# Reordering the merge of a triangular inverse: both halves' steps one and two first, then step three of the second half alternating with step four of the first

## The reference, cut to what matters

```python
M = jnp.tril(M, k=-1)
kexp = kg * jnp.exp(Gg)[:, :, :, None, :]
rhs = (vg - jnp.einsum('bhtid,bhdv->bhtiv', kexp, S)).reshape(b, h, C * Rr, dv)
u = jax.scipy.linalg.solve_triangular(M, rhs, lower=True, unit_diagonal=True)
...
S_new = jnp.exp(glast)[..., None] * S + jnp.einsum('bhtid,bhtiv->bhdv', kdec, u)
```

## Time and profile before

| | |
|---|---|
| runs of the kernel | 5012.32, 5018.0, 5028.32 us (median 5018.0) |
| span of the profiled execution | 5005.7 us |
| PE busy | 4517.9 us (90%), 63200 matmul records |
| PE weight loads | 3131.9 us (63%), beside the matmuls |
| DVE busy | 4134.4 us (83%) |
| ACT busy | 3484.7 us (70%) |
| POOL busy | 3217.8 us (64%) |
| DMA | mean 27 GB/s, queue 1 at 7.2% of 16 engines |

### The profile page before, as it was taken

How to read it: one execution, slowest core, us unless ns; L and a number is a source line. 1 busy time by engine, 2 the same in 40 slices (tenths; PEclk the granted TensorE clock), 3 DMA queues, 4 the chain that set the end, 5 groups by cost and what they waited for, 6 DMA issues and landing times.

```text
span 5005.7 us, 151432 instructions
## 1 busy us (share of the span) xinstructions
PE 4517.9 (90%) x63200; PEld 3131.9 (63%) x63200; DVE 4134.4 (83%) x7262; ACT 3484.7 (70%) x6775; POOL 3217.8 (64%) x5316
## 2 busy tenths in 40 slices
PE   8869999999999999999999999899999999999888
PEld 5536666666666666666666666666666666666655
DVE  3289998888988899889998899888998899988622
ACT  3367777777777777777777777777777777777531
POOL 0047777776777777777777777777777777777600
PEclk9979999999999999999999999999999999999899
DMA  2200000000000000000100000000000000000100
GB/s 88 94 21 21 25 25 25 16 22 25 34 32 15 28 25 25 25 14 25 34 32 28 15 25 25 25 16 23 30 29 25 14 24 25 25 25 8 38 9 21
DMA packets 49724, 135.45 MB, mean 27 GB/s; under 512 B 7056, under 2 KB 28176, under 8 KB 48400
## 3 DMA queue, kind: packets, MB, share of 16 engines
q1 hardware_dynamic: 49040, 125.77, 7.2%
HBM read 111.60 MB, written 14.16 MB: 25 GB/s over the span
## 4 chain that ended last, share of the span: by engine, by line
PE 54%; DVE 26%; ACT 11%; issue 7%; POOL 1%; DMA 0%; DVEq 0%; SPq 0%; ACTq 0%
PE bank L835 46%; DVE acc L1557 8%; PE bank L302 7%; DVE X L1554 7%; DVE sp_t L1554 2%; ACT L1432 2%; DVE Pd L1662 2%; ACT Us L1181 2%; ACT o L1182 1%; DVE Zc L1741 1%; DVE Rs L1557 1%; DVE o L1557 1%; ACT acc L1181 1%; PE bank L906 1%; DVE x1m L1554 1%
## 5 line engine op out<-in xcount | busy, mean ns | idle before, releaser
L1557 DVE SCALAR_TENSOR_TENSOR acc<-bank,vc,acc 128x510 f32<-128x510 f32 (+2 forms) x1728 | 1272.9, 740 | 148.5 <-ACT acc L1181 122.9
L2002 POOL TENSOR_TENSOR LZ<-LZ,LT 128x120 f32<-128x120 f32 (+26 forms) x1984 | 957.3, 483 | 155.5
L1999 POOL TENSOR_TENSOR LT<-LA,LZ 128x120 f32<-128x120 f32 (+26 forms) x1984 | 917.1, 462 | 145.9
L1554 DVE TENSOR_TENSOR X<-KQ,Fl 128x640 f32<-128x640 f32 x1024 | 1002.8, 995 | 1.5 <-ACT Fl L1182 1.5
L1972 POOL COPY X<-KQ 128x640 f32<-128x640 f32 x256 | 246.4, 962 | 912.4 <-PE bank L835 312.2
L835 PE MATMUL bank<-X 128*32 128x60 f32 (+1 forms) x32768 | 650.8, 205 | 132.6 <-DVE Pd L1662 85.9
L835 PEld LDWEIGHTS bank<-X 128*32 128x32 f32 x32768 | 524.7, 112 | 369.1 <-issue 211.0
L1181 ACT ACTIVATE Us<-bank 128x128 f32<-128x128 f32 x1024 | 281.2, 276 | 621.3 <-PE bank L835 615.2
L835 PE MATMUL bank<-xnTm,WK 128*128 128x512 f32 x1280 | 662.7, 643 | 42.0 <-DVE acc L1557 36.3
L835 PE MATMUL bank<-Rs,Ztf 128*128 128x128 f32 x2048 | 467.4, 314 | 68.8 <-DVE Rs L1557 48.6
L1951 POOL TENSOR_TENSOR kdec<-KQ,Fe 128x512 f32<-128x512 f32 x256 | 336.8, 1316 | 299.4 <-PE bank L906 299.4
(11 more groups left out here) (145 smaller groups left out, 9346.4 us busy)
## 6 DMA issues: line engine op xcount, KB each, us to landing
WK<-in_wkq SPq DMA_DIRECT2D x64, 704.0 KB, 5.9
WV<-in_wv SPq DMA_DIRECT2D x64, 576.0 KB, 3.8
WO<-in_wo SPq DMA_DIRECT2D x64, 128.0 KB, 2.0
wuh<-in_wu SPq DMA_DIRECT2D x2, 1024.0 KB, 7.4
xt<-in_x SPq DMA_DIRECT2D x4, 512.0 KB, 6.2
wuh_d<-wuh SPq DMA_DIRECT2D x1, 2048.0 KB, 6.3
x_d<-x SPq DMA_DIRECT2D x4, 512.0 KB, 3.1
xnT_d<-xT SPq DMA_DIRECT2D x4, 512.0 KB, 2.7
```

What stands on the lines that cost most here:

```text
L1554: return e.tensor_tensor(o, a, b, op)
L1557: return e.scalar_tensor_tensor(out=o, in0=a, scalar=sc, in1=b, op0=op0, op1=op1)
L1999: e.tensor_tensor(tmp, LA[:, j + 1:32, 8 * (j % R) + j // R].unsqueeze(2).broadcast_to([P, rr, cc]), LZ[:, j, 0:cc].unsqueeze(1).broadcast ...
L2002: e.tensor_tensor(LZ[:, j + 1:32, 0:cc], LZ[:, j + 1:32, 0:cc], tmp, SUB).then_inc(g_row, 1)
```

## The change

On PE and on ACT the calls of the merge for stage `p-2` stand in another order; `third` and `fourth` on PE become three functions, one of which, `third_fourth`, issues a matmul of the third step of half 1 and one of the fourth step of half 0 in turn. The waits are written anew for this order. What is computed, the number of matmuls, their shapes and the copies on ACT are the same. DVE, GpSimd and the queues are not edited.

```diff
                 w.wait_ge(a_E, every(s, 8))
-                w.wait_ge(a_Z, nth(s, 2, hb - 1))
-                w.wait_ge(a_Y4, nth(s, 2, hb - 1))
+                w.wait_ge(a_Z, every(s - 1, 2))
+                w.wait_ge(a_W, nth(s, 6, 3 * hb - 1))
...
                 w.wait_ge(a_Ys, nth(s, 2, hb))
+                w.wait_ge(a_W, nth(s, 6, 3 * hb - 1))
...
+            def third_of(s, u):
+                return mm(bank[4][64:128, 64 * (u % 8):64 * (u % 8) + 64],
+                          E[0:64, s % 2, u, 1:3].rearrange("p g c -> p (g c)"), Zc[0:64, u, :])
+
+            def fourth_of(s, u):
+                return mm(bank[4][0:64, 64 * (u % 8):64 * (u % 8) + 64], Y4[64:128, u % 8, :], Ztf[64:128, u, 64:128])
+
+            def third(s):
...
+                w.wait_ge(a_W, every(s, 6))
                 for c in range(8):
-                    u = 8 * hb + c
-                    ins = mm(bank[4][64:128, 64 * c:64 * c + 64], E[0:64, s % 2, u, 1:3].rearrange("p g c -> p (g c)"),
-                             Zc[0:64, u, :])
+                    ins = third_of(s, c)
                 ins.then_inc(p_inv[2], 1)
...
+            def third_fourth(s):
...
+                w.wait_ge(a_Y4, nth(s, 2, 0))
                 for c in range(8):
-                    u = 8 * hb + c
-                    ins = mm(bank[4][0:64, 64 * c:64 * c + 64], Y4[64:128, c, :], Ztf[64:128, u, 64:128])
+                    ins = third_of(s, 8 + c)
+                    if c == 7:
+                        ins.then_inc(p_inv[2], 1)
+                    ins = fourth_of(s, c)
+                ins.then_inc(p_inv[3], 1)
+
+            def fourth(s):
...
+                w.wait_ge(a_Y4, every(s, 2))
+                w.wait_ge(a_Z, nth(s, 2, 0))
+                for c in range(8):
+                    ins = fourth_of(s, 8 + c)
                 ins.then_inc(p_inv[3], 1)
```

The list on PE (the list on ACT has the same moves, with `third(p - 2, 1)` and `fourth(p - 2, 0)` where PE has `third_fourth`):

```diff
                 products(p - 1, 2, 4)
-                third(p - 2, 0)
+                first(p - 2, 1)
                 spare(p - 2, 32)
                 turn_v(p - 2, 2)
                 turn(p - 1, 0)
-                fourth(p - 2, 0)
+                second(p - 2, 1)
                 spare(p - 2, 33)
                 total(p)
                 turn_v(p - 2, 3)
                 products(p - 1, 3, 0)
-                first(p - 2, 1)
+                third(p - 2)
                 spare(p - 2, 34)
                 products(p - 1, 3, 1)
                 turn(p - 1, 1)
-                second(p - 2, 1)
+                third_fourth(p - 2)
                 spare(p - 2, 35)
                 products(p - 1, 3, 2)
                 products(p - 1, 3, 3)
                 solve(p - 2, 0, 0)
                 products(p - 1, 3, 4)
                 project_k(p + 1, 0)
-                third(p - 2, 1)
+                fourth(p - 2)
                 spare(p - 2, 36)
                 update(p - 2, 0, 0)
                 project_k(p + 1, 1)
-                fourth(p - 2, 1)
```

ACT's copies of `first` and `third` get one wait more each, for the PE group that still reads `Ys` or `Y4`:

```diff
                 w.wait_ge(p_inv[0], nth(s, 2, hb))
+                w.wait_ge(p_inv[1], nth(s, 2, hb - 1))
...
                 w.wait_ge(p_inv[2], nth(s, 2, hb))
+                w.wait_ge(p_inv[3], nth(s, 2, hb - 1))
```

More of the change, by code:

```diff
@@ L966, in second @@
                 ins.then_inc(p_inv[1], 1)
-            def third(s, hb):
+            def third_of(s, u):
[4 more added lines that the diff above has]
+            def third(s):
                 if not 0 <= s < NS:
                     return
-                w.wait_ge(a_W, nth(s, 6, 3 * hb + 2))
+                w.wait_ge(a_W, every(s, 6))
                 for c in range(8):
-                    u = 8 * hb + c
-                    ins = mm(bank[4][64:128, 64 * c:64 * c + 64], E[0:64, s % 2, u, 1:3].rearrange("p g c -> p (g c)"),
-                             Zc[0:64, u, :])
+                    ins = third_of(s, c)
                 ins.then_inc(p_inv[2], 1)
-            def fourth(s, hb):
+            def third_fourth(s):
                 if not 0 <= s < NS:
                     return
-                w.wait_ge(a_Y4, nth(s, 2, hb))
+                w.wait_ge(a_Y4, nth(s, 2, 0))
                 for c in range(8):
-                    u = 8 * hb + c
-                    ins = mm(bank[4][0:64, 64 * c:64 * c + 64], Y4[64:128, c, :], Ztf[64:128, u, 64:128])
+                    ins = third_of(s, 8 + c)
[4 more added lines that the diff above has]
+            def fourth(s):
+                if not 0 <= s < NS:
+                    return
+                w.wait_ge(a_Y4, every(s, 2))
+                w.wait_ge(a_Z, nth(s, 2, 0))
+                for c in range(8):
+                    ins = fourth_of(s, 8 + c)
                 ins.then_inc(p_inv[3], 1)
@@ L1507, in delta_scalar @@
                 silu_v(p - 1, 2)
-                first(p - 2, 1)
+                third(p - 2, 0)
                 rhs(p - 2, 0, 0)
@@ L1514, in delta_scalar @@
                 turned(p - 1, 1)
-                second(p - 2, 1)
+                third(p - 2, 1)
+                fourth(p - 2, 0)
                 root(p, 1)
@@ L1520, in delta_scalar @@
                 tap_k(p + 1, 0)
-                third(p - 2, 1)
+                fourth(p - 2, 1)
                 factors(p, 0)
```

## The result

The changed kernel takes 5200.9 us (median of 4 runs, 5197.87 to 5218.64) against 5016.3 us: a ratio of 1.0369, 95% interval 1.0345 to 1.0394, slower. The forecast was 5170 us, 5085 to 5235. The profiled execution took 5202.57 us at a span of 5200.7, 195.0 more than the span before.

A forecast was written before the change was run, and what follows sets the result against it. No engine bounds the whole; who waits last at each place counts. 63 steps x 2.2 = 139 us on the 5005.7 span, plus 12.3 for the median and 13 for the clock, gives 5170 us, range 5085 to 5235.

The forecast's parts named there:

- PE ahead of products(3,0) is covered: PE reaches products(3,0) 0.88 us sooner but waits for DVE's `Pd`; idle grows from 1.43 to 2.3 us, worth nothing.
- ACT sets the start of solve(0,0): ACT's four steps take 5.25 us before solve(0,0) is released, so PE waits there 1.6 to 2.5 us.
- The alternating group at 1.3 us, between 1.26 and 2.14: Time on PE of third(1) alternating with fourth(0); the sum does not depend on where in these bounds it lies.
- +2.2 us a stage: DVE empties products(3,4) 2.2 us later, shifting `Rs`; all engines leave the place about 2.2 us late, 139 us over 63 steps.
- The other way through the stage: With fourth(1) ahead of update(0,0) and the second projection, rhs(0,1) and solve(1,0) come 1.9 to 2.2 us later.
- The clock: 8 more falls, 13 us: Two PE idle waits within 7 us cause 8 more costly clock falls, 13 us; bounds none to 101 us.
- The rival of a fall in nearly every stage: Two long waits close together make the clock fall in nearly every stage: plus 101 us, 5258 us; chance 0.10.
- PE's saving: Rival: ACT does not hold solve(0,0), so PE's saving gains 0.52 us a stage: 4985 us; chance 0.06.
- Half absorbed: Rival: DVE or ACT regain about 1.1 us a stage: 5087 us; chance 0.09.
- The order holds the solve: Denied by the no-change rival: the order does not hold solve(0,0), ACT's wait being met earlier, 5018 us; chance 0.04.
- 1.9 a stage without a fall: Low end of the forecast's own range, 5130 us: only PE's shift at solve(1,0) counts and no clock fall.

The follow-up runs named there:

- e1_two_blocks: The changed kernel, but the eight matmuls of third(1) come first and then the eight of fourth(0), not in turn: 5230.5 us.
- e3_copies_first: The changed kernel with ACT's copies of third(1) and fourth(0) moved ahead of the table load, first root and kdT: 5067.1 us.
- e2_solve_behind: The changed kernel with solve(0,0) moved behind products(3,4) on PE: 5127.6 us.
- e5_fill_both: The changed kernel with added matmuls nobody reads, eight ahead of products(3,0) and eleven ahead of solve(0,0): 5175.4 us.
- e7: The kernel before in its own order, with one added wait of solve(0,0) on PE for ACT's second root: 5337.9 us.
- e8_late_early: The changed kernel with both repairs, solve(0,0) behind products(3,4) on PE and ACT's two copies ahead of the table load: 5087.6 us.

## Why the prediction was right, step by step

- *PE ahead of products(3,0) is covered.* Right: 2.06 us of idle time (2.3 forecast), still behind `Pd`, and products(3,0) keeps its place in the stage. PE comes 0.63 us earlier and not 0.88, as a wait of 0.20 us for DVE's `acc` now stands further ahead in its list; that is worth nothing either way.
- *ACT sets the start of solve(0,0).* Right, and shown by two runs: lengthening PE's part moves nothing (steady stage of e1_two_blocks), shortening ACT's part by 2.0 us brings solve(0,0) forward by 2.0 (e3_copies_first). ACT's 5.25 us measured 5.39 (2134.41 to 2139.80), for its unchanged piece took 3.51 us instead of 3.37; solve(0,0) starts 7.13 us after products(3,0), forecast 6.98. PE idles 2.70 us there, a little over the 1.6 to 2.5 forecast.
- *The alternating group at 1.3 us, between 1.26 and 2.14.* It took 1.08, below the lower bound. That bound took the time of the first step as proportional to its columns; sixteen matmuls of 32 columns take 0.63 us and sixteen of 64 columns 1.08, less than twice as long. The sum didn't hang on it. The Trainium skill, "TensorEngine Tiling (Array Packing)", restrictions and gotchas, says that different row tiles cannot access one PSUM bank at the same time. If that is taken to mean that such matmuls run one after the other, it does not hold here, where the two of a pair write different partition halves of bank 4: 1.08 us for sixteen matmuls, against 1.07 for eight of the same size in one tile.
- *+2.2 us a stage.* Mis-sized by 0.26: +2.46. Of it 0.15 is the later release and 0.10 the step from solve(0,0) to products(3,4), taken at 0.32 and measured at 0.42 (2140.22 - 2139.80), for which the forecast had named 0.17 as the risk. 155 us instead of 139. DVE's idle time ahead of products(3,4) was forecast at about 2 us and measured 3.44: DVE was ready 1 us earlier than before (its `rn<-C` ends 4.90 us after products(3,0), before 5.94), as the `X` operation ahead of it took 0.79 us, before 1.83. GpSimd's `kdec` ran beside nearly all of the longer one and beside little of the shorter one; no run changes that alone. It too only lengthened a wait. The other way through the stage came out as forecast: rhs(0,1) starts 13.58 us after products(3,0), forecast 13.5 to 13.7, before 11.40. e2_solve_behind shows that this way costs 1.56 us a stage even where DVE isn't held at products(3,4).
- *The clock: 8 more falls, 13 us.* This is the term that was sized worst. Net 25 more falls in 58 stages (47 against 22), and stages 0.52 us further above their steady length, 33 us in all; e5_fill_both, which takes 33 of the early falls away, wins 26. The forecast took the projection 5 us behind the old wait as the nearest row, where one wait stood and now there are two. Early falls are 5 with 1.43 us at products(3,0) alone, 26 with 2.04 and 0.72 at solve(0,0), 36 with 2.04 and 2.18, 42 with 2.06 and 2.70, and 59 with 1.43 and 3.39 (the kernel before, e3, e2, the changed kernel, e7). But with one of the two filled they are still 37 or 46, so the sum of the waits isn't the rule; which rule holds is open. The rival of a fall in nearly every stage was right in the count, 40 of 58 stages with a fall in that part, and three times too dear, 101 us. Two reasons are likely, neither shown: falls went away elsewhere (17 to 5), and part of the slow time lies under the wait for ACT. The Trainium skill, "TensorE: Matmul & The Clock Gate", in the section on HAM oscillation, describes a kernel with a wait of 3 to 5 us in each round that starts each round at the slow clock; here two waits of 2.06 and 2.70 us did so in most stages.
- *The rivals.* PE's saving does not count, not even with both repairs (e8_late_early, 5087.6, with 4950 to 4990 as the rival's number). Half absorbed did not happen: the stage grows by as much as `Rs` comes late. The order holds the solve. Two sums are slightly off: by the forecast's own steps PE's saving reaches rhs(0,1) at 73.54 and not 73.49 (30 us in all, not 33), and 1.9 a stage without a fall gives 5138, not 5130. Nothing hangs on either.

The sum came out 31 us low: 16 from the step, 20 from the clock and 7 in the stages outside the 58, less 12. The last is luck. The forecast added 12.3 us because the median before lies that far above the profiled span; after, the two differ by 0.2.

## What to carry to other kernels

When a chain of copies is moved closer to its first use, add up what stands on the copying engine between the result and the use, not what the producing engine saves; here 1.1 us of overlap was bought with 5.3 us of ACT's list in front of the engine that feeds all others. Moving the two copies ahead of unrelated work was worth 134 us, more than any change of the matmuls. An idle wait of TensorE has a second price, the clock: count falls before and after, and try filling waits with matmuls that nobody reads before reordering anything. Fill all neighbouring waits together, since one alone gained nothing here and once cost 32 us.

## What was not expected of the hardware

- Behind idle waits as short as 0.45 and 0.81 us, ahead of a stretch of small matmuls, the clock fell for mostly 10 to 17 us (0.72 and 0.70 granted in the windows above), and with the 0.81 filled these falls were gone. The 1.43 us at products(3,0) of the kernel before went with 5 falls in 58 stages.
- Filling a wait with matmuls that do nothing useful makes the kernel faster: 34 to 39 us for eleven matmuls a stage. Filling one of the two neighbouring waits in the changed kernel did not.
- Sixteen 64 x 64 matmuls that alternate between two disjoint row and column halves of the array take 1.08 us, as long as eight in one of them (1.07); and with the two blocks in series the second block's first matmul starts before the first block's last ones, so that 1.83 us are taken instead of 2.14.
